# One matmul for gate and up, maxima and exps split by side over three banks each, and the residual add ahead of its maximum

## The chip, the cores and the metric

The kernel runs on one core of one Trainium2 chip. The metric is the device time of one launch in microseconds. TensorE does the matmuls, VectorE, ScalarE and GpSimd the elementwise work, and SyncE issues most DMAs. In the profile they are PE (PEld are its weight loads), DVE, ACT, POOL and SP.

## The reference

One adaLN transformer block over 16 batches of 512 tokens of width 128:

```python
mod = (silu(c) @ wmod).reshape(16, 6, 1, 128)
h = layernorm(x) * (1 + ca) + sa
x = x + ga * attention(h)      # 16 heads of width 8, softmax over 512 keys
h = layernorm(x) * (1 + cb) + sb
x = x + gb * moe(h)            # 8 experts, top 2, hidden width 176
```

The attention is `softmax((h Wq + bq)(h Wk + bk)^T / sqrt(8)) (h Wv + bv)`, then `Wo` and `bo`. An expert is `(silu(h wg) * (h wu)) wd`, and a token's two results are weighted by a softmax over its two best router scores.

## The kernel before, in words

**Attention.** A batch has 16 heads, worked in 4 groups of 4. Two heads make a pair, a "side" each, on rows 0 to 63 and 64 to 127 of TensorE's array. For each pair and each of the 4 tiles of 128 tokens there is a half slot. It has a *score* step two groups ahead of the rest (L808: two matmuls, one for each side, 128 queries by 512 keys; VectorE takes the row maxima of both sides at L1267) and an *exp* step (L817: the two matmuls again, turned and with the maxima as an extra term; ScalarE takes exp at L1038). So there are 32 half slots in a batch. Two of them make one of the 16 slots `k`, and `slot(b, k)` in each engine's program is that engine's share.

TensorE's slot is, in order: scores and exps of half 0, one "misc" step of that slot, scores and exps of half 1, the *value* matmuls (L835, eight records, the weighted sum of the group before), and after every fourth slot the transposed maxima ("shift", L746). `misc_at` says which misc step stands where: slots 1, 5, 9, 13 turn the group's output ("o", L750), 2 the routing places, 3 h2T (L764), 4 v (L742), 6 the router scores (L767), 7 oT, 8 y (L757), 10 x1 (L760), 11 hT (L735), 12 q (L737), 14 k (L739); 0 and 15 have none. All misc steps share bank 7 of PSUM, and each waits until the one before it is drained, mostly by ScalarE between its exps (h_t L995, q and k L999, v_aug L1002, o_t L1004, h2_t L1006, z L1009, shift_n L1017, o_s L1020, and the copy of the value bank, o_aug, L1034). x1 is drained by VectorE: `take_x1` (L1175) adds x into `x1_s`.

**Banks.** PSUM has 8 banks of 512 fp32 columns. Scores use banks 0 to 3 as two areas of two banks, by half slot. Exps use banks 4 and 5 as one area. Bank 6 is for values, bank 7 for misc. TensorE waits before a score step until all maxima but the last step's are done, and before an exp step until all exps are done. The order of work is fixed by the program of each engine. Semaphores `scores_ready`, `maxes_done`, `st_ready`, `exps_done` tie them.

**VectorE beside the maxima.** From slot 6 to slot 11 of a batch it has 16 small router steps of an earlier batch, two per half slot. In slot 11 it has four `bn_stats`.

**Experts.** After attention the 8192 tokens, sorted by expert with GpSimd's indirect DMAs, are worked in 144 tiles of 128 rows: turn the rows (L876), gate and up (L883, two matmuls of 176 columns with the same stationary operand), silu (L1081), product (L1392), turn the hidden rows (L892), down (L900), results back by indirect DMA (L1606). Leftover misc steps of the last batch are mixed into the first tiles. The two halves of the batches are two "superblocks"; the second waits until all its rows are placed.

Of the kernel before, what the change touches and what calls it, by code (L numbers as in the profile page):

```python
# [60 lines left out]
RSTD, NMR, CA, SA, GA, GABO = 0, 4, 8, 9, 10, 11  # L61
PV_BANK, MISC_BANK = 6, 7
XT_BANK, GU_BANK, HT_BANK, Y_BANK = 0, 1, 3, 4
EXP_AREA = 2
STEPS = NH * QT // 2
AHEAD_STEPS = 16

# [57 lines left out]
def along(eng, sem, f, q, d):  # L125

    v = f(q) if d is None else d * (f(q + 1) - f(q)) + f(q)
    if not isinstance(v, int) or v > 0:
        eng.wait_ge(sem, v)

def rows_by_four(v):
# [28 lines left out]
def adaln_block(nc, x, Wq, bq, Wk, bk, Wv, bv, Wo, bo, gate_w, wg, wu, wd, c, wmod,  # L162
                ident_c, tri_c, rank_c, slots_c, map_c, place_c, out):
    with ExitStack() as ctx:
# [36 lines left out]
        mod = sb("mod", [P, 3, NB])  # L201
        gtmp = sb("gtmp", [P, 3, NB])
        row_s = sb("row_s", [NB, ROW_N])
        wg_t = sb("wg_t", [P, NC, P])
        wu_t = sb("wu_t", [P, NC, P])
        wd_t = sb("wd_t", [HALF, 2 * NE, D])
        prm = sb("prm", [P, NB, PRM])
        mv = sb("mv", [P, NT, 2])
# [481 lines left out]
        def _(pe):  # L690
# [37 lines left out]
            def misc_step(kind, n, g, d):  # L728
# [13 lines left out]
                        mm = pe.matmul(misc[:, P * t:P * (t + 1)], h_t[:, P * t:P * (t + 1)], wvT,  # L742
                                       start=True, stop=True)
                elif kind == "shift":
                    wait(pe, maxes_done, lambda n: 2 * GROUP * (NG * n + g + 1), n, d)
                    mm = pe.transpose(misc[0:4 * QT, 0:P], maxes[g % 2][:, :, :, :].rearrange("p a c q -> p (a c q)"), ident[:, :])  # L746
                elif kind == "o":
                    wait(pe, pv_taken, lambda n: NG * n + g + 1, n, d)
# [45 lines left out]
            def slot(b, k, d=None):  # L794
                    g, hh = divmod(k, GROUP)
                    s = NG * b + g
                    exps, looks = 0 <= s < NS, 0 <= s + 2 < NS
                    j, js, bs = 2 * g + hh // 2, (2 * g + hh // 2 + GROUP) % PAIRS, b + (g + 2) // NG
                    for half in range(2):
                        t, step = 2 * (hh % 2) + half, 2 * k + half  # L800
                        if looks:
                            if k == 8 and half == 0:
                                for i in range(2):
                                    wait(pe, stacked[i], lambda b: 16 * STACK_DMAS * (b + 2), b, d)
                            wait(pe, maxes_done, lambda b: STEPS * b + step + AHEAD_STEPS - 1, b, d)
                            for side in range(2):
                                rows = slice(SIDE * side, SIDE * side + SHIFT)
                                mm = pe.matmul(ps[:, 2 * half + side, :], q_st[bs % 2][rows, js, P * t:P * (t + 1)],  # L808
                                               k_st[bs % 2][rows, js, :], start=True, stop=True)
                            mm.then_inc(scores_ready, 1)  # L810
                        if exps:
                            if hh == 0 and half == 0:
                                wait(pe, shift_stacked, lambda b: 32 * (NG * b + g + 1), b, d)
                            wait(pe, exps_done, lambda b: STEPS * b + step, b, d)
                            for side in range(2):
                                rows = slice(SIDE * side, SIDE * side + SHIFT + 2)
                                mm = pe.matmul(ps[:, 2 * EXP_AREA + side, :], k_st[b % 2][rows, j, P * t:P * (t + 1)],  # L817
                                               q_st[b % 2][rows, j, :], start=True, stop=True)
                            mm.then_inc(st_ready, 1)
                        if half:  # L820
                            weigh_values(b, g, hh, d)
                        misc_steps(b, k, half, d)

            def weigh_values(b, g, hh, d):

                s = NG * b + g
                if 0 <= s - 1 < NS:
                    gp, bp = (g - 1) % NG, b + (g - 1) // NG
                    if hh == 0:
                        wait(pe, exps_done, lambda b: 2 * GROUP * (NG * b + g), b, d)  # L830
                        wait(pe, pv_taken, lambda b: NG * b + g - 1, b, d)
                        if gp == 0:
                            wait(pe, misc_drained, lambda b: at["v", b] + 1, b, d)
                    for i in range(GROUP):
                        mm = pe.matmul(ps[VW * i:VW * (i + 1), PV_BANK, :], v_aug[bp % 2][:, hh, GROUP * gp + i, :],  # L835
                                       probs[:, gp % 2, i, S * hh:S * (hh + 1)], start=(hh == 0), stop=(hh == QT - 1))
                    if hh == QT - 1:
                        mm.then_inc(pv_ready, 1)
# [28 lines left out]


            pe.wait_ge(map_step, MAP_STEPS)
            pe.wait_ge(exps_done, STEPS * NB)  # L870

            def turn_rows(m, q, d):

# [4 lines left out]
            def up(m, q, d, e):  # L878

                along(pe, xt_taken, lambda q: PAIR * q + m + 1, q, d)  # L880
                along(pe, hid_ready, lambda q: PAIR * q + m - 1, q, d)
                for i, w in enumerate((wg_t, wu_t)):
                    mm = pe.matmul(ps[:, GU_BANK + m % 2, INTER * i:INTER * (i + 1)], x_t[m % 2],  # L883
                                   w[:, :, :].rearrange("p c h -> p (c h)")[:, bass.ds(e * INTER, INTER)],
                                   start=True, stop=True)
                mm.then_inc(gu_ready, 1)

            def turn_hidden(m, q, d):
                along(pe, hid_ready, lambda q: PAIR * q + m + 1, q, d)
# [61 lines left out]
        def _(act):  # L951
# [20 lines left out]
            def ffn_weights():  # L972
                act.wait_ge(setup_filled, SETUP_MOD2 + 1)
                act.copy(mod_r[:, :, :].rearrange("p a d -> p (a d)"), ps[0:NB, SETUP_MOD2 % 2, 0:3 * D]).then_inc(setup_drained, 1)
                for i, (w, c0, n, width) in enumerate(FFN_GROUPS):
                    act.wait_ge(setup_filled, SETUP_FFN + i + 1)
                    act.copy((wg_t, wu_t, wd_t)[w][:, c0:c0 + n, :].rearrange("p k d -> p (k d)"),
                             ps[0:width, (SETUP_FFN + i) % 2, 0:P * n]).then_inc(setup_drained, 1)

            def prm_of(n):  # L980
# [43 lines left out]
            def slot(b, k, d=None):  # L1024
                    g, hh = divmod(k, GROUP)
                    s = NG * b + g
                    for half in range(2):
# [7 lines left out]
                        if 0 <= s < NS:  # L1035
                            pair_at = 2 * (hh // 2)
                            wait(act, st_ready, lambda b: STEPS * b + step + 1, b, d)
                            act.activation(probs[:, g % 2, pair_at:pair_at + 2, S * t:S * (t + 1)],  # L1038
                                           ps[:, 2 * EXP_AREA:2 * EXP_AREA + 2, :], ACT.Exp, scale=SCALE).then_inc(exps_done, 1)
                        other = misc_at(b, k, half)  # L1040
                        if other and other[0] in ("hT", "q", "k", "v", "oT", "y", "h2T"):
                            misc_drain(*other, d)
# [60 lines left out]
        def _(dve):  # L1103
# [144 lines left out]
            def slot(b, k, d=None):  # L1248
# [3 lines left out]
                    for t in range(QT):  # L1252
                        spot = QT * k + t
                        if 0 <= b - 1 < NB:
# [3 lines left out]
                            if spot == AGGR_AT:  # L1258
                                wait(dve, x1_stats, lambda b: 4 * b, b, d)
                                wait(dve, h2_ready, lambda b: b - 1, b, d)  # L1260
                        if looks and t % 2 == 0:
                            step, tile = 2 * k + t // 2, 2 * (hh % 2) + t // 2
                            area = step % 2
                            if hh == 0 and t == 0 and s >= 0:
                                wait(dve, misc_filled, lambda b: at["shift", NG * b + g] + 1, b, d)
                            wait(dve, scores_ready, lambda b: STEPS * b + step + AHEAD_STEPS + 1, b, d)
                            dve.tensor_reduce(maxes[g % 2][:, :, hh // 2, tile:tile + 1], ps[:, 2 * area:2 * area + 2, :],  # L1267
                                              AX.X, ALU.max).then_inc(maxes_done, 1)
                        other = (misc_at(b, k, 0) if t == 2 else misc_at(b, k - 1, 1) if t == 0 and k else None)
                        if other and other[0] == "x1":  # L1270
                            take_x1(other[1], d)
                        elif other and other[0] == "o":
                            invert_sums(other[1] // NG, other[1] % NG, d)
                        if 0 <= b - 1 < NB:
                            if k == STATS_AT:
# [378 lines left out]
```

## Time and profile before

| | us |
|---|---|
| median of 3 runs | 1164.21 (1160.67 to 1167.68) |
| the profiled execution, own time | 1163.8 |
| its span | 1161.6 |
| PE busy | 985.4 (85%) |
| DVE busy | 865.3 (74%) |
| ACT busy | 794.5 (68%) |
| POOL busy | 677.7 (58%) |

The profile lists busy time by engine, the chain of work that ended last, groups of instructions by line with the idle time before them, and each instruction's start and duration. Attention fills the span to about 877 us, the experts the rest to about 1131, and then come the last sums. "xN" behind a row is how many records are merged in it.

### The profile page before, as it was taken

Reading aid. Unit: us, or ns where it says so; the run is one execution under the profiler, and the core shown is the slowest. Engines: PE = TensorE matmul, PEld = TensorE weight load, DVE = VectorE, ACT = ScalarE, POOL = GpSimd, SP = SyncE. Lnnn points to the kernel's source line nnn. Section 1 sums busy time; section 2 is a strip of 40 time slices with the busy share of each in tenths; the row PEclk is TensorE's granted clock in tenths of the full one; section 3 lists DMA queues with packets and bytes.
Section 4 is the critical chain, followed back from the end, with each engine's and each line's share of the span. In section 5 each row is a group of like instructions: output and inputs, shape, how many; then the busy total and the mean of one; then the engine's idle time right before and its main releaser. Section 6 shows DMA issues by size and latency. Waiting matters only on the chain.

```text
span 1161.6 us, 24273 instructions
## 1 busy us (share of the span) xinstructions
PE 985.4 (85%) x6746; PEld 458.0 (39%) x6747; DVE 865.3 (74%) x1586; ACT 794.5 (68%) x1296; POOL 677.7 (58%) x938
## 2 busy tenths in 40 slices
PE   4778889899898989989898988989788989799990
PEld 2212223223232332323232332323225888689980
DVE  7867788798888979888887978888842554355555
ACT  2367788788778878778787777878675655355550
POOL 6414162857567484856648485664436877765663
PEclk9779999999999999999999999999999999899995
DMA  8211121313112121211122121212022333455566
GB/s 254 76 53 39 38 66 37 84 52 103 51 57 65 56 81 35 83 51 56 52 69 81 35 81 44 65 41 71 11 60 66 81 87 82 123 159 156 168 228 222
DMA packets 98602, 96.32 MB, mean 83 GB/s; under 512 B 21861, under 2 KB 77778, under 8 KB 98514
## 3 DMA queue, kind: packets, MB, share of 16 engines
q1 hardware_dynamic: 89810, 77.34, 23.7%
q0 software_dynamic: 8704, 17.97, 4.5%
q8 instruction: 35, 0.57, 0.2%
q14 instruction: 53, 0.43, 0.1%
HBM read 40.91 MB, written 28.60 MB: 60 GB/s over the span
## 4 chain that ended last, share of the span: by engine, by line
PE 60%; ACT 15%; issue 10%; DVE 7%; SPq 3%; DMA 3%; DVEq 1%; POOL 0%; ACTq 0%
PE ps L835 18%; ACT probs L1038 14%; PE ps L817 11%; PE ps L808 8%; PE ps L883 7%; PE ps L900 5%; PE ps L892 3%; DVE maxes L1267 2%; PE ps L742 1%; PE ps L739 1%; PE ps L737 1%; PE ps L767 1%; PE ps L876 1%; DMA ys_d<-probs,k_st 1%; PE ps L757 1%
## 5 line engine op out<-in xcount | busy, mean ns | idle before, releaser
L1267 DVE TENSOR_REDUCE maxes<-ps 128x2 f32<-128x1024 f32 x512 | 614.3, 1221 | 121.9 <-PE ps L808 116.7
L1038 ACT ACTIVATE probs<-ps 128x1024 f32<-128x1024 f32 x512 | 524.0, 1023 | 152.9 <-PE ps L817 151.0
L835 PE MATMUL ps<-probs,v_aug 128*32 128x512 f32 x2048 | 273.3, 606 | 0.8 <-ACT o_aug L1034 0.8
L817 PE MATMUL ps<-q_st,k_st 64*128 64x512 bf16 x1024 | 200.1, 387 | 79.2 <-ACT probs L1038 77.7
L808 PE MATMUL ps<-k_st,q_st 62*128 62x512 bf16 x1024 | 203.5, 394 | 10.2 <-DVE maxes L1267 9.2
L1493 POOL TENSOR_TENSOR shift_h<-shift_n,one 16x128 bf16<-16x128 f32 x64 | 24.9, 389 | 234.7 <-ACT shift_n L1017 234.7
L1539 POOL DMA_INDIRECT xs_d<-h,rows_o x128 | 125.2, 978 | 35.9 <-issue 35.9
L1388 DVE COPY probs<-ps 88x256 f32<-88x256 f32 x144 | 60.4, 420 | 110.2 <-PE ps L892 107.8
L808 PEld LDWEIGHTS ps<-k_st,q_st 62*128 62x128 bf16 x1024 | 49.3, 93 | 234.8 <-DVE maxes L1267 133.5
L817 PEld LDWEIGHTS ps<-q_st,k_st 64*128 64x128 bf16 x1024 | 50.9, 93 | 175.9 <-ACT probs L1038 147.0
L900 PE MATMUL ps<-wd_t,probs 88*128 x576 | 92.4, 284 | 0.0
L1606 POOL DMA_INDIRECT ys_d<-probs,q_st x72 | 69.7, 969 | 35.6 <-ACT probs L1087 25.9
L1077 ACT COPY probs<-ps 128x128 f32<-128x128 f32 x143 | 38.0, 266 | 74.1 <-PE ps L876 71.1
L1606 POOL DMA_INDIRECT ys_d<-probs,k_st x72 | 70.9, 985 | 29.0 <-ACT probs L1087 17.7
L883 PE MATMUL ps<-wg_t,probs 128*128 x288 | 74.1, 340 | 8.9 <-issue 4.0
L900 PEld LDWEIGHTS ps<-wd_t,probs 88*128 88x128 f32 x576 | 77.2, 195 | 2.9 <-issue 0.2
L1502 POOL TENSOR_TENSOR o_n<-o_s,o_rs 128x128 f32<-128x128 f32 x64 | 27.0, 422 | 86.8 <-DVE o_rs L1167 81.5
L883 PE MATMUL ps<-wu_t,probs 128*128 x288 | 67.9, 318 | 0.0
L835 PEld LDWEIGHTS ps<-probs,v_aug 128*32 128x32 f32 x2048 | 40.4, 108 | 67.8 <-issue 66.1
L892 PE MATMUL ps<-ident,probs 128*88 128x128 f32 x288 | 56.5, 278 | 8.5 <-DVE probs L1392 5.4
L1392 DVE TENSOR_TENSOR probs<-probs,ps 128x176 f32<-128x176 f32 x144 | 46.6, 324 | 10.3 <-ACT probs L1081 10.2
L883 PEld LDWEIGHTS ps<-wu_t,probs 128*128 128x128 f32 x288 | 50.5, 196 | 0.0
(218 smaller groups left out, 1314.5 us busy)
## 6 DMA issues: line engine op xcount, KB each, us to landing
q_st<-q_parts SPq DMA_DIRECT2D x96, 128.0 KB, 2.4
k_st<-k_parts SPq DMA_DIRECT2D x96, 128.0 KB
probs<-ys_d SPq DMA_DIRECT2D x24, 256.0 KB, 3.3
q_st<-xs_d SPq DMA_DIRECT2D x72, 65.0 KB
k_st<-xs_d SPq DMA_DIRECT2D x72, 65.0 KB, 1.9
probs<-L_attn_x SPq DMA_DIRECT2D x4, 1024.0 KB, 8.9
x_r<-L_attn_x SPq DMA_DIRECT2D x16, 256.0 KB, 2.8
x_d<-x_s SPq DMA_DIRECT2D x16, 256.0 KB, 2.1
```

The source lines that it names most:

```text
L808: mm = pe.matmul(ps[:, 2 * half + side, :], q_st[bs % 2][rows, js, P * t:P * (t + 1)], k_st[bs % 2][rows, js, :], start=True, stop=True)
L817: mm = pe.matmul(ps[:, 2 * EXP_AREA + side, :], k_st[b % 2][rows, j, P * t:P * (t + 1)], q_st[b % 2][rows, j, :], start=True, stop=True)
L835: mm = pe.matmul(ps[VW * i:VW * (i + 1), PV_BANK, :], v_aug[bp % 2][:, hh, GROUP * gp + i, :], probs[:, gp % 2, i, S * hh:S * (hh + 1)], s ...
L883: mm = pe.matmul(ps[:, GU_BANK + m % 2, INTER * i:INTER * (i + 1)], x_t[m % 2], w[:, :, :].rearrange("p c h -> p (c h)")[:, bass.ds(e * IN ...
L892: mm = pe.transpose(ps[0:HALF, HT_BANK, P * i:P * (i + 1)], hid[m % 2][:, HALF * i:HALF * (i + 1)], ident[:, :])
L900: mm = pe.matmul(ps[:, Y_BANK + m % 2, 0:D], hid_t[m % 2][:, P * i:P * (i + 1)], wd_t[:, bass.ds(e * 2 + i, 1), :].rearrange("p a d -> p ( ...
L1038: act.activation(probs[:, g % 2, pair_at:pair_at + 2, S * t:S * (t + 1)], ps[:, 2 * EXP_AREA:2 * EXP_AREA + 2, :], ACT.Exp, scale=SCALE).t ...
L1267: dve.tensor_reduce(maxes[g % 2][:, :, hh // 2, tile:tile + 1], ps[:, 2 * area:2 * area + 2, :], AX.X, ALU.max).then_inc(maxes_done, 1)
L1388: dve.tensor_copy(hid_t[(m - 1) % 2], ps[0:HALF, HT_BANK, 0:2 * P]).then_inc(hidt_taken, 1)
L1392: dve.tensor_tensor(hid[m % 2], silu[m % 2], ps[:, GU_BANK + m % 2, INTER:2 * INTER], ALU.mult).then_inc(hid_ready, 1)
L1539: pool.indirect_dma_start(xs_d, bass.IndirectOffsetOnAxis(ap=rows_o[:, v:v + 1], axis=0), h2[n % 2][:, v // QT, v % QT, :], None).then_inc ...
L1606: pool.indirect_dma_start(ys_d, bass.IndirectOffsetOnAxis(ap=x_in[m % SLOTS][:, D + 1:XW].bitcast(U32), axis=0), y_out[m % SLOTS], None).t ...
```

## The change

Three edits. (1) Each score and exp step keeps its two matmuls, but the maxima and the exps are taken in one instruction for each side, of 512 columns instead of 1024. Side 0 of the scores always lands in bank 0, side 1 in banks 1 and 2 by turns; exps likewise in banks 3, 4 and 5. TensorE waits for a score step until side 0 of the step before and side 1 of the one before that are done, and for exps likewise. (2) The gate and up weights lie in one tile `wgu_t`, and one matmul of 352 columns (two runs of 176) takes both. (3) `take_x1` stands ahead of its half slot's maximum, not behind it.

```diff
+SCORE_BANK, EXP_BANK = 0, 3
+def bank_of(first, side, step):
+    return first + 1 + step % 2 if side else first
...
-                            wait(pe, maxes_done, lambda b: STEPS * b + step + AHEAD_STEPS - 1, b, d)
+                            wait(pe, maxes_done, lambda b: 2 * (STEPS * b + step + AHEAD_STEPS) - 1, b, d)
                             for side in range(2):
...
-                                mm = pe.matmul(ps[:, 2 * half + side, :], q_st[bs % 2][rows, js, P * t:P * (t + 1)],
+                                mm = pe.matmul(ps[:, bank_of(SCORE_BANK, side, step), :], q_st[bs % 2][rows, js, P * t:P * (t + 1)],
...
-                            wait(pe, exps_done, lambda b: STEPS * b + step, b, d)
+                            wait(pe, exps_done, lambda b: 2 * (STEPS * b + step) - 1, b, d)
...
-                for i, w in enumerate((wg_t, wu_t)):
-                    mm = pe.matmul(ps[:, GU_BANK + m % 2, INTER * i:INTER * (i + 1)], x_t[m % 2],
-                                   w[:, :, :].rearrange("p c h -> p (c h)")[:, bass.ds(e * INTER, INTER)],
-                                   start=True, stop=True)
-                mm.then_inc(gu_ready, 1)
+                pe.matmul(ps[:, GU_BANK + m % 2, 0:2 * INTER].rearrange("p (a h) -> p a h", a=2), x_t[m % 2],
+                          wgu_t[:, :, :, :].rearrange("p a c h -> p a (c h)")[:, :, bass.ds(e * INTER, INTER)],
+                          start=True, stop=True).then_inc(gu_ready, 1)
...
-                            act.activation(probs[:, g % 2, pair_at:pair_at + 2, S * t:S * (t + 1)],
-                                           ps[:, 2 * EXP_AREA:2 * EXP_AREA + 2, :], ACT.Exp, scale=SCALE).then_inc(exps_done, 1)
+                            for side in range(2):
+                                act.activation(probs[:, g % 2, pair_at + side, S * t:S * (t + 1)],
+                                               ps[:, bank_of(EXP_BANK, side, step), :], ACT.Exp, scale=SCALE).then_inc(exps_done, 1)
...
+                        x1 = misc_at(b, k, 0) if t == 2 else None
+                        if x1 and x1[0] == "x1":
+                            take_x1(x1[1], d)
                         if looks and t % 2 == 0:
...
-                            dve.tensor_reduce(maxes[g % 2][:, :, hh // 2, tile:tile + 1], ps[:, 2 * area:2 * area + 2, :],
-                                              AX.X, ALU.max).then_inc(maxes_done, 1)
+                            for side in range(2):
+                                dve.tensor_reduce(maxes[g % 2][:, side, hh // 2, tile:tile + 1],
+                                                  ps[:, bank_of(SCORE_BANK, side, step), :], AX.X, ALU.max).then_inc(maxes_done, 1)
```

The waits on `maxes_done` and `exps_done` elsewhere count twice as much.

On VectorE, around slot 10 of a batch, the maxima (L1267 before, L1274 now) and the residual add `x_s` (L1175, now L1179) stand as follows. Before:

```order
L1223 TENSOR_TENSOR top<-top 128x4
L118 REGISTER_ALU
L1267 TENSOR_REDUCE maxes<-ps 128x2
L118 REGISTER_ALU x3
L1175 TENSOR_TENSOR x_s<-ps,x_r 128x512
```

Now:

```order
L1227 TENSOR_TENSOR top<-top 128x4
L118 REGISTER_ALU x3
L1179 TENSOR_TENSOR x_s<-ps,x_r 128x512
L118 REGISTER_ALU
L1274 TENSOR_REDUCE maxes<-ps 128x1 x2
```

The add has moved in front of the half slot's maximum, and that is now two instructions, one for each side.

On TensorE, one expert tile among the first (`probs` holds the turned rows, `ISA` and `REGISTER_ALU` are waits and address work). Before:

```order
L883 ISA
L883 MATMUL ps<-wg_t,probs 128x176
L883 REGISTER_ALU
L883 MATMUL ps<-wu_t,probs 128x176
L876 MATMUL ps<-ident,k_st 128x128
```

Now:

```order
L887 ISA
L887 MATMUL ps<-wgu_t,probs 128x352
L881 MATMUL ps<-ident,k_st 128x128
```

Two matmuls and one address step have become one matmul; what stands around them is as it was.

## Rows read from the trace of the kernel before

**Rows 1.** The page's chain that ended last, by engine and by line.

```profile
PE 60%; ACT 15%; issue 10%; DVE 7%; SPq 3%; DMA 3%; DVEq 1%; POOL 0%; ACTq 0%
PE ps L835 18%; ACT probs L1038 14%; PE ps L817 11%; PE ps L808 8%; PE ps L883 7%; PE ps L900 5%; PE ps L892 3%; DVE maxes L1267 2%; PE ps L742 1%; PE ps L739 1%; PE ps L737 1%; PE ps L767 1%; PE ps L876 1%; DMA ys_d<-probs,k_st 1%; PE ps L757 1%
```

**Rows 2.** Busy us of PE, PEld, DVE, ACT, POOL over two batch periods.

```profile
350.85:402.09 51.24, 46.18 (x322) 15.20 (x321) 44.06 (x65) 40.65 (x53) 32.36 (x48) 1.00 0.22 61
95.80:146.10 50.30, 44.30 (x302) 13.37 (x302) 39.26 (x38) 40.17 (x51) 15.74 (x22) 1.00 0.16 46
```

**Rows 3.** The line of h_t, one instruction per batch: durations, first and last start.

```profile
L995 ACT ACTIVATE h_t<-ps,prm_a x15: 774/777/781, 45.0 to 759.5; 128x512 f32<-128x512 f32 x15
```

**Rows 4.** Timeline (start, duration, engine, line), slots 2 and 3 of one batch.

```profile
372.03 1.06 PE L835 MATMUL ps<-probs,v_aug 128*32 128x512 f32 x8
...
373.02 0.39 PE L808 MATMUL ps<-k_st,q_st 62*128 62x512 bf16 x2
...
373.25 0.38 PE L817 MATMUL ps<-q_st,k_st 64*128 64x512 bf16 x2
...
373.46 2.36 DVE L1267 TENSOR_REDUCE maxes<-ps 128x2 f32<-128x1024 f32 x2 [0.59 <-PE ps L808]
...
373.67 1.02 ACT L1038 ACTIVATE probs<-ps 128x1024 f32<-128x1024 f32 x1 [0.51 <-PE ps L817]
...
374.15 0.39 PE L808 MATMUL ps<-k_st,q_st 62*128 62x512 bf16 x2
...
374.59 0.58 ACT L1006 COPY h_t<-ps 128x512 f32<-128x512 f32 x1
...
374.75 0.39 PE L817 MATMUL ps<-q_st,k_st 64*128 64x512 bf16 x2 [0.21 <-ACT probs L1038]
...
375.18 1.02 ACT L1038 ACTIVATE probs<-ps 128x1024 f32<-128x1024 f32 x1
```

**Rows 5.** Timeline of DVE, slots 7 to 12 of the same batch.

```profile
385.99 1.23 DVE L1267 TENSOR_REDUCE maxes<-ps 128x2 f32<-128x1024 f32 x1 [0.21 <-PE ps L808]
387.13 0.18 DVE L1205 TENSOR_REDUCE top<-route 128x4 f32<-128x32 f32 x1
...
388.58 1.64 DVE L1209 TENSOR_TENSOR route<-route,rank 128x32 f32<-128x32 f32 x1
...
399.09 0.68 DVE L1175 TENSOR_TENSOR x_s<-ps,x_r 128x512 f32<-128x512 f32 x1
...
403.31 1.23 DVE L1267 TENSOR_REDUCE maxes<-ps 128x2 f32<-128x1024 f32 x1
```

**Rows 6.** Timeline of PE, slot 11.

```profile
399.90 0.65 PE L735 MATMUL ps<-ident,x_n 128*128 128x128 f32 x4 [1.20 <-DVE x_s L1175]
```

**Rows 7.** The chain in order of time (start, length, what).

```profile
37.50 8.02 DVE maxes L1267 x7
...
351.59 1.05 PE ps L737 x2
...
376.68 1.09 PE ps L742 x8
...
857.89 0.41 PE ps L817 x2
...
859.40 0.41 PE ps L817 x2
...
1060.83 0.64 PE ps L883 x4
...
1062.24 0.64 PE ps L883 x4
```

**Rows 8.** Groups by line and shape, 200 to 800 us.

```profile
L1267 DVE TENSOR_REDUCE maxes<-ps 128x2 f32<-128x1024 f32 x376 | 452.2, 1221 | 83.8 <-PE ps L808 79.2 <-issue 2.0
L1038 ACT ACTIVATE probs<-ps 128x1024 f32<-128x1024 f32 x376 | 384.8, 1023 | 101.1 <-PE ps L817 99.4
...
L1175 DVE TENSOR_TENSOR x_s<-ps,x_r 128x512 f32<-128x512 f32 x11 | 7.5, 680 | 0.0
```

More of the change, by code:

```diff
@@ L63 @@
 XT_BANK, GU_BANK, HT_BANK, Y_BANK = 0, 1, 3, 4
-EXP_AREA = 2
+SCORE_BANK, EXP_BANK = 0, 3
 STEPS = NH * QT // 2
@@ L203, in adaln_block @@
         row_s = sb("row_s", [NB, ROW_N])
-        wg_t = sb("wg_t", [P, NC, P])
-        wu_t = sb("wu_t", [P, NC, P])
+        wgu_t = sb("wgu_t", [P, 2, NC, P])
         wd_t = sb("wd_t", [HALF, 2 * NE, D])
@@ L744, in misc_step @@
                 elif kind == "shift":
-                    wait(pe, maxes_done, lambda n: 2 * GROUP * (NG * n + g + 1), n, d)
+                    wait(pe, maxes_done, lambda n: 4 * GROUP * (NG * n + g + 1), n, d)
                     mm = pe.transpose(misc[0:4 * QT, 0:P], maxes[g % 2][:, :, :, :].rearrange("p a c q -> p (a c q)"), ident[:, :])
@@ L813, in slot @@
                                 wait(pe, shift_stacked, lambda b: 32 * (NG * b + g + 1), b, d)
-                            wait(pe, exps_done, lambda b: STEPS * b + step, b, d)
+                            wait(pe, exps_done, lambda b: 2 * (STEPS * b + step) - 1, b, d)
                             for side in range(2):
                                 rows = slice(SIDE * side, SIDE * side + SHIFT + 2)
-                                mm = pe.matmul(ps[:, 2 * EXP_AREA + side, :], k_st[b % 2][rows, j, P * t:P * (t + 1)],
+                                mm = pe.matmul(ps[:, bank_of(EXP_BANK, side, step), :], k_st[b % 2][rows, j, P * t:P * (t + 1)],
                                                q_st[b % 2][rows, j, :], start=True, stop=True)
@@ L829, in weigh_values @@
                     if hh == 0:
-                        wait(pe, exps_done, lambda b: 2 * GROUP * (NG * b + g), b, d)
+                        wait(pe, exps_done, lambda b: 4 * GROUP * (NG * b + g), b, d)
                         wait(pe, pv_taken, lambda b: NG * b + g - 1, b, d)
@@ L869, in _ @@
             pe.wait_ge(map_step, MAP_STEPS)
-            pe.wait_ge(exps_done, STEPS * NB)
+            pe.wait_ge(exps_done, 2 * STEPS * NB)
             def turn_rows(m, q, d):
@@ L976, in ffn_weights @@
                     act.wait_ge(setup_filled, SETUP_FFN + i + 1)
-                    act.copy((wg_t, wu_t, wd_t)[w][:, c0:c0 + n, :].rearrange("p k d -> p (k d)"),
+                    act.copy((wd_t if w == 2 else wgu_t[:, w, :, :])[:, c0:c0 + n, :].rearrange("p k d -> p (k d)"),
                              ps[0:width, (SETUP_FFN + i) % 2, 0:P * n]).then_inc(setup_drained, 1)
@@ L1260, in slot @@
                                 wait(dve, h2_ready, lambda b: b - 1, b, d)
+                        x1 = misc_at(b, k, 0) if t == 2 else None
+                        if x1 and x1[0] == "x1":
+                            take_x1(x1[1], d)
                         if looks and t % 2 == 0:
                             step, tile = 2 * k + t // 2, 2 * (hh % 2) + t // 2
-                            area = step % 2
                             if hh == 0 and t == 0 and s >= 0:
@@ L1266, in slot @@
                             wait(dve, scores_ready, lambda b: STEPS * b + step + AHEAD_STEPS + 1, b, d)
-                            dve.tensor_reduce(maxes[g % 2][:, :, hh // 2, tile:tile + 1], ps[:, 2 * area:2 * area + 2, :],
-                                              AX.X, ALU.max).then_inc(maxes_done, 1)
+                            for side in range(2):
+                                dve.tensor_reduce(maxes[g % 2][:, side, hh // 2, tile:tile + 1],
+                                                  ps[:, bank_of(SCORE_BANK, side, step), :], AX.X, ALU.max).then_inc(maxes_done, 1)
                         other = (misc_at(b, k, 0) if t == 2 else misc_at(b, k - 1, 1) if t == 0 and k else None)
-                        if other and other[0] == "x1":
-                            take_x1(other[1], d)
-                        elif other and other[0] == "o":
+                        if other and other[0] == "o":
                             invert_sums(other[1] // NG, other[1] % NG, d)
```

## The prediction

> **What bounds the kernel now.** First the chain that ended last [rows 1]: TensorE holds 60% of it (values, exps' and scores' matmuls in front), the exps 14%, the maxima 2%. Then the batch as a unit: h_t comes once per batch, from 45.0 to 759.5 us in 15 instructions, so a period is 714.5 / 14 = 51.0 us [rows 3]. In a late one of 51.24 us PE is busy 46.18, DVE 44.06, ACT 40.65 [rows 2]. No engine is full, so the loss is in handshakes, and the three loads lie so close together that a gain in one soon meets the next.
>
> The handshake is in one slot [rows 4]. With its start (373.02) as 0: scores at 0, exps' matmuls 0.23, maxima 0.44, exp 0.65, misc step 0.54, second scores 1.13. The second exps' matmuls need the exp (1.02) done and start only at 1.73, the values 0.32 later, and they hold PE for 0.99 (372.03 to 373.02): about 3.05 in all. PE idles because exps have one area. Where the misc step is long (q 1.05, v 1.09 [rows 7]) it covers that wait, and such a slot lasts 0.54 + 1.07 + 0.54 + 0.99 = 3.14 already.
>
> Slots 7 to 11 are another regime. DVE starts a maximum of slot 7 at 385.99 and that of slot 12 at 403.31 [rows 5]: 17.32 us for ten maxima with the router's steps between them, one right behind another. There DVE is the bound. PE's wait of 1.20 us for `x_s` at 399.90 [rows 6] lies inside that stretch.
>
> **The price of two instructions for one.** DVE: a maximum of 1024 columns lasts 1.221, and the nearest row of 512 columns out of PSUM is the add, 0.680 [rows 8]. So half a maximum is about 0.68. In a stream the next instruction starts 0.08 before the end of the one in front: 387.13 - 385.99 = 1.14 for 1.23 [rows 5], and two maxima take 2.36, not 2.46 [rows 4]. Two halves take 2 x (0.68 - 0.08) = 1.20 against 1.14, +0.06 a half slot. Bounds: 0 (a half is just half) and 2 x 0.68 - 1.14 = +0.22 (no overlap at all). I take 0.06, since the overlap shows between maxima and between a maximum and small steps alike.
>
> ACT: an exp lasts 1.023 [rows 8], the nearest of 512 columns, the h2_t copy, 0.58, and it starts at 374.59, 0.10 before the exp of 373.67 ends [rows 4]. A pair of half exps is 2 x 0.59 - 0.10 = 1.08, +0.06. Bounds 0 and +0.16.
>
> The rows show a fixed part of about 0.14 in a maximum, of which 0.06 is left in a stream. The Trainium skill (VectorE: DVE Perf Modes, section on the TRN2 errata) puts it at 120 cycles of 0.96 GHz for an operand in PSUM, and says that many small tiles pay it each: an estimated 0.125 us for each added maximum. By that price the result would be near the first rival's.
>
> **What the banks give.** TensorE now waits for side 0 of the step before only. From one exps' matmul to the next: 0.42 until ACT starts (373.25 to 373.67), 0.59 for side 0, 0.05 for the signal, 1.06; it was 1.50. From one score step to the next: 0.44 + 0.68 + 0.05 = 1.17. That is a new limit. Before, PE could be a whole step ahead of DVE, now half of one. Behind a waiting score step stand the exps' matmuls, values and the misc step, which ACT, DVE and the copy of the value bank wait for, so each slot has to be followed on all three engines.
> - A plain slot (13, 15, 1, 2, 3, 5): second scores at 1.17, exps' matmuls at 1.39 (the exp's side 0 ended at 1.24), values at 1.71, end 2.70. Was 3.05: -0.35. DVE needs 2.40 in it, ACT 2 x 0.98. Six of them: -2.1.
> - Slot 0: ACT copies the value bank (0.59) before its first exp, so the second exps' matmuls start at 1.45, plus the shift 0.21: 2.95. With slot 15 it was 6.43, now 5.65; beyond the plain gain of 15 that is -0.4.
> - Slots 6 and 14: PE 3.1 as before, 0.
> - Slot 4: ACT has 1.96 + 0.49 + 0.49 + 0.17 (exps, copy, v, shift) = 3.1 in a slot of 3.37; 0.
> - Slot 12: DVE comes out of slot 11 0.8 behind, so the second scores start at 1.22 + 0.73 = 1.95, not 1.6: 3.7, was 3.53, +0.2.
> - Slots 7 to 11: DVE is the bound, ten half slots by 0.06: +0.6.
> That makes -1.7. The following assumes that no wait meets another, so I take -1.4 a batch, between that and the -1 that is left if every plain slot loses another 0.1. Against DVE's load: 44.06 + 32 x 0.06 = 46.0 of 49.7, no contradiction.
>
> **x ahead of its maximum.** The same DVE work in another order, in the stretch that DVE bounds. PE's hT starts earlier, but its next scores wait for DVE anyway, and the maximum behind the add ends 0.6 later. I take 0; bounds +0.3 and -1.2 a batch, the whole wait of [rows 6].
>
> **Gate and up in one.** Between two tiles lie 1.41 us (1060.83, 1062.24), and gate and up hold 0.64 of it [rows 7]. Four matmuls of 128 columns (v) took 1.09 and one of 512 (q) 1.05 [rows 7]: 0.013 for each matmul saved. Its two passes of records go too, so I take 0.02 x 144 tiles = -3. Bounds: by proportion to the 1.05 of 512 columns the 352 would take 0.72, +0.08 a tile, +12; at best all four records save 0.013, -7. Nothing hides it, since PE bounds the tiles; where the second superblock's rows are waited for, a gain before that is lost.
>
> **The sum**, on the profiled execution's 1163.8 us (span 1161.6), which is 0.4 below the median of 1164.2 and stands for it:
> - 13 periods, slot 11 of batch 1 to slot 11 of batch 14, by 1.4: -18.
> - Two periods before them have no router steps; DVE is busy 39.26 of 50.30 there [rows 2], so slots 7, 9, 10, 11 and 12 gain as plain ones do: 2 x 3.3 = -7.
> - Last batch: slots 12 to 6, -2.2. From slot 8 on no scores are left and the exps alone bound, 857.89 to 859.40, 1.51 a half slot [rows 7]. Now a slot is 1.06 + 0.4 + 0.99 = 2.46, was 3.02: eight times, -4.4.
> - Experts: -3.
> - The first 16 maxima stand alone, 8.02 for 7, 1.15 each [rows 7]; the handshake makes that 1.17 at least, and more at the lower granted clock there: +3.
> Together -31: 1133.
>
> **Rivals.**
> *Halves don't overlap each other*: +0.14 on DVE, +0.16 on ACT a half slot. Slots 7 to 11 lose 1.4, slot 4 and 5 lose 0.4 because ACT runs behind, plain slots keep 0.3: 0 a batch. 1163.8 - 5 - 4 - 3 + 3 = 1155. For it: two instructions on neighbouring banks are not among the pairs that the trace shows. Against: every pair that it does show overlaps.
> *DVE pays the full price*, 0.22: 44.06 + 32 x 0.22 = 51.1 busy; with 1.5 us of idle at score waits 52.6 a period, +1.6. 13 x 1.6 = +21, start +5, last batch -4, experts -3: 1183. It decides from about +0.14 a half slot on. Against it the same rows.
> *The wait for `x_s` is real*: if hT holds slots 11 and 12, another -1.2 a batch, -17: 1116. Against: behind 399.09 DVE has no idle time.
> *Half a step ahead is too little*: what PE no longer waits for ACT it waits for DVE, whose small steps fall between maxima: 1160. For it: DVE's 17.3 us stretch; against: DVE is idle 7 us a period.
>
> **Chances.** Forecast's case (1122 to 1146) 0.50; halves don't overlap 0.18; `x_s` 0.10; too little ahead 0.11; full price 0.11. Less than 0.5% (6 us) can't be told from no change here. Faster: 0.50 + 0.10 + 0.15 of the first rival = 0.75; within: 0.14; slower: 0.11. The range goes from 1114, the `x_s` case, to 1162, past the first and the last rival.
>
> **What would show it.** Half maxima of 0.68 and pairs of 1.28 on DVE; half exps of 0.59, pairs of 1.08; slots 2 and 3 at 2.7, with the second scores waiting for a maximum; slot 7 to 12 on DVE at 18.0; h_t every 49.6; the last batch's exps at 1.2 a half slot; gate and up at 0.62 in a tile of 1.39. The forecast is wrong if h_t still comes every 51 us, if a pair of halves takes 1.36, or if PE's waits for maxima grow by what its waits for exps shrink.

## The result

The changed kernel takes 1146.13 us (median of 4 runs, 1145.74 to 1148.6), the kernel before 1164.22 on the same chip: a ratio of 0.985, with a 95% interval of 0.982 to 0.988. That is 18 us saved. The forecast was 31 us (1133); the time lies inside its range (1114 to 1162), at the very edge of the likeliest case's own (1122 to 1146). The profiled execution took 1146.32, its span 1144.1 against 1161.6, so 17.5 us went out of the span. The ratios with intervals in this text are taken from fast runs alone, and can differ by up to 0.4% from the quotient of the medians beside them.

### The profile after

The page's chain that ended last, as in [rows 1]:

```profile
PE 43%; DVE 20%; issue 13%; POOL 12%; SPq 4%; DMA 4%; ACT 3%; DVEq 1%; POOLq 0%; ACTq 0%
```

GpSimd (POOL) had no share in the chain of before. It has 12% now, and with it SyncE and a DMA. The groups of instructions (busy time and mean ns of one, then the idle time in front and what ended it), first TensorE's two of the kernel before:

```profile
L817 PE MATMUL ps<-q_st,k_st 64*128 64x512 bf16 x1024 | 200.1, 387 | 79.2 <-ACT probs L1038 77.7
L808 PE MATMUL ps<-k_st,q_st 62*128 62x512 bf16 x1024 | 203.5, 394 | 10.2 <-DVE maxes L1267 9.2
```

and of the changed one:

```profile
L1274 DVE TENSOR_REDUCE maxes<-ps 128x1 f32<-128x512 f32 x1024 | 647.7, 683 | 81.4 <-PE ps L813 71.9
L1042 ACT ACTIVATE probs<-ps 128x512 f32<-128x512 f32 x1024 | 559.6, 603 | 128.3 <-PE ps L822 123.7
...
L813 PE MATMUL ps<-k_st,q_st 62*128 62x512 bf16 x1024 | 205.6, 398 | 79.5 <-DVE maxes L1274 76.9
L822 PE MATMUL ps<-q_st,k_st 64*128 64x512 bf16 x1024 | 199.0, 385 | 14.1 <-ACT probs L1042 8.9
```

A half maximum lasts 0.683 us, a half exp 0.603. The matmuls of the scores (L813) now wait for maxima (76.9 us, 9.2 before), and those of the exps (L822) hardly for anything (8.9 us for exps, 77.7 before). Most slots are as forecast. The timeline of slot 15 of one batch, to set beside [rows 4]:

```profile
453.88 1.07 PE L840 MATMUL ps<-probs,v_aug 128*32 128x512 f32 x8
...
454.88 0.39 PE L813 MATMUL ps<-k_st,q_st 62*128 62x512 bf16 x2
455.11 0.38 PE L822 MATMUL ps<-q_st,k_st 64*128 64x512 bf16 x2
455.31 1.89 DVE L1274 TENSOR_REDUCE maxes<-ps 128x1 f32<-128x512 f32 x3 [0.25 <-PE ps L813]
455.53 1.78 ACT L1042 ACTIVATE probs<-ps 128x512 f32<-128x512 f32 x3 [0.34 <-PE ps L822]
456.06 0.39 PE L813 MATMUL ps<-k_st,q_st 62*128 62x512 bf16 x2 [0.57 <-DVE maxes L1274]
456.29 0.38 PE L822 MATMUL ps<-q_st,k_st 64*128 64x512 bf16 x2
456.60 0.64 PE L840 MATMUL ps<-probs,v_aug 128*32 128x512 f32 x4
```

With the slot's start (454.88) as 0: second scores at 1.18, exps' matmuls at 1.41, values at 1.72. From one run of value matmuls to the next it is 456.60 - 453.88 = 2.72, against 3.05 before. The forecast said 1.17, 1.39, 1.71 and 2.70.

And yet the batch gained less than the plain slots promise. The line of h_t, one per batch, as in [rows 3]:

```profile
L998 ACT ACTIVATE h_t<-ps,prm_a x15: 777/783/784, 46.7 to 751.2; 128x512 f32<-128x512 f32 x15
```

The mean period is (751.2 - 46.7) / 14 = 50.3 us, where 51.0 was before and 49.6 was forecast. Two waits that were in no row of before take the difference. The first is on ScalarE, at the start of its loop's body (slot 0 of every second batch; the loop has five rounds, and so four jumps back):

```profile
459.49 0.59 ACT L1037 COPY o_aug<-ps 128x512 f32<-128x512 f32 x1 [1.69 <-issue]
...
460.63 0.39 PE L822 MATMUL ps<-q_st,k_st 64*128 64x512 bf16 x2 [1.46 <-ACT probs L1042]
```

ScalarE sits idle for 1.69 us with nothing that the profile shows to wait for ("issue"), and TensorE then waits 1.46 for its exps. This comes 4 times in the trace, at rounds two to five, 1.54 to 1.79 us each. At the place before, the same copy followed the exp in front of it at once (363.84, behind an exp of 362.74 that lasted 1.02).

The second is in slot 4. The exps' matmuls of a batch's next group need the shift that comes by DMA from GpSimd's `shift_l`. The chain in order of time:

```profile
514.35 1.17 POOL h L1489
...
515.78 0.97 issue
516.74 1.18 POOL h L1492
517.92 0.35 POOL shift_h L1498
...
518.35 0.43 POOL shift_l L1501
...
518.79 0.56 SPq L506
...
519.39 1.61 DMA q_st<-shift_l
...
521.04 0.39 PE ps L822 x2
```

GpSimd's second layer norm (`h`) stands in front of the shift, the shift in front of the DMA, and TensorE stands behind it all. From the start of the shift before it to the end of this one GpSimd takes 18.2 us in both kernels, one instruction right behind the other (406.16 to 424.34 in a batch before, 500.58 to 518.77 here), while TensorE's slots beside it have become shorter. The same layer norm already holds TensorE one slot earlier, at the transposes of h2T, which waited 9 times and 3.9 us in all for `h`:

```profile
517.97 0.66 PE L769 MATMUL ps<-ident,h 128*128 128x128 f32 x4 [0.47 <-POOL h L1492]
```

Over the whole run (idle time of PE and PEld before L822):

```profile
  ACT probs L1042: 28.7, 36
  DMA q_st<-shift_l: 11.5, 17
```

In the trace of before that second releaser doesn't occur at L817: only ACT and "issue" do. Nor does the wait for `h`.

### Where the 17.5 us are

| part of the span | before | after | change | forecast |
|---|---|---|---|---|
| start to the first h_t | 45.0 | 46.7 | +1.7 | +3 |
| 14 periods between h_t | 714.5 | 704.5 | -10.0 | -23 |
| last h_t to the end, without the experts' tiles | 124.2 | 118.2 | -6.0 | -8 |
| experts, first tile to the end | 277.9 | 274.7 | -3.2 | -3 |

The third row is 402.1 - 277.9 and 392.9 - 274.7. The last h_t stands in slot 11 of batch 13, so of the forecast's 15 periods 14 lie between the h_t (2 x 3.3 + 12 x 1.4 = 23.4), and the last belongs to the third row (1.4 + 2.2 + 4.4 = 8.0). The periods missed most of it, by 13 us. The first three gained 0.9, 3.9 and 1.5, the eleven behind them 0.3 on average, and two of those came to 52.4 and 52.3, longer than any of before (51.3).

### The profile page after: what moved, and what is told of

The parts are those of the page before. It is cut to its first block, busy times and chain, and to the rows that moved or that the text cites. A ratio compares the mean times of both kernels' runs of the same rounds, so it can differ in the third digit from the quotient of the medians.

```text
span 1144.1 us, 24592 instructions
## 1 busy us (share of the span) xinstructions
PE 971.6 (85%) x6458; PEld 399.0 (35%) x6459; DVE 894.0 (78%) x2098; ACT 808.0 (71%) x1808; POOL 677.8 (59%) x938
## 4 chain that ended last, share of the span: by engine, by line
PE 43%; DVE 20%; issue 13%; POOL 12%; SPq 4%; DMA 4%; ACT 3%; DVEq 1%; POOLq 0%; ACTq 0%
DVE maxes L1274 15%; PE ps L840 10%; PE ps L813 7%; PE ps L887 6%; PE ps L903 5%; PE ps L822 4%; PE ps L895 3%; POOL rest L1461 2%; ACT probs L1042 2%; PE ps L755 2%; PE ps L747 2%; PE ps L772 1%; DMA q_st<-shift_l 1%; PE ps L881 1%; DVE st_b L1282 1%
## 5 line engine op out<-in xcount | busy, mean ns | idle before, releaser
L1274 DVE TENSOR_REDUCE maxes<-ps 128x1 f32<-128x512 f32 x1024 | 647.7, 683 | 81.4 <-PE ps L813 71.9
L1042 ACT ACTIVATE probs<-ps 128x512 f32<-128x512 f32 x1024 | 559.6, 603 | 128.3 <-PE ps L822 123.7
L813 PE MATMUL ps<-k_st,q_st 62*128 62x512 bf16 x1024 | 205.6, 398 | 79.5 <-DVE maxes L1274 76.9
L822 PE MATMUL ps<-q_st,k_st 64*128 64x512 bf16 x1024 | 199.0, 385 | 14.1 <-ACT probs L1042 8.9
L813 PEld LDWEIGHTS ps<-k_st,q_st 62*128 62x128 bf16 x1024 | 49.4, 93 | 339.6 <-DVE maxes L1274 323.8
L887 PE MATMUL ps<-wgu_t,probs 128*128 x288 | 116.2, 485 | 8.9 <-issue 4.0
L822 PEld LDWEIGHTS ps<-q_st,k_st 64*128 64x128 bf16 x1024 | 51.2, 95 | 33.9 <-ACT probs L1042 19.8
L887 PEld LDWEIGHTS ps<-wgu_t,probs 128*128 128x128 f32 x288 | 43.7, 191 | 11.8 <-issue 11.7
L1085 ACT ACTIVATE probs<-ps 128x176 f32<-128x176 f32 x144 | 46.5, 323 | 0.3 <-PE ps L887 0.3
```

Source lines behind the costliest of these rows:

```text
L813: mm = pe.matmul(ps[:, bank_of(SCORE_BANK, side, step), :], q_st[bs % 2][rows, js, P * t:P * (t + 1)], k_st[bs % 2][rows, js, :], start=Tr ...
L822: mm = pe.matmul(ps[:, bank_of(EXP_BANK, side, step), :], k_st[b % 2][rows, j, P * t:P * (t + 1)], q_st[b % 2][rows, j, :], start=True, st ...
L887: pe.matmul(ps[:, GU_BANK + m % 2, 0:2 * INTER].rearrange("p (a h) -> p a h", a=2), x_t[m % 2], wgu_t[:, :, :, :].rearrange("p a c h -> p ...
L1042: act.activation(probs[:, g % 2, pair_at + side, S * t:S * (t + 1)], ps[:, bank_of(EXP_BANK, side, step), :], ACT.Exp, scale=SCALE).then_i ...
L1274: dve.tensor_reduce(maxes[g % 2][:, side, hh // 2, tile:tile + 1], ps[:, bank_of(SCORE_BANK, side, step), :], AX.X, ALU.max).then_inc(maxe ...
```

## The experiments

They ran on three chips. On two of them every kernel is slower, the one before too (1241.27 and 1257.44 against 1163 to 1164), so only ratios to the kernel before on the same chip are compared. All edits are against the kernel before unless it says otherwise.

### First four: each part by itself

**Gate and up alone.** The edit is the merged matmul of the diff ahead, with `wgu_t` for the two tables.

> The kernel before with the merged gate and up matmul alone. In the trace of the full change the steady tile still takes 1.41 us and gate and up still hold TensorE for 0.64. Theory: TensorE is bound by the 352 streamed columns, not by the number of matmuls, so the steady tile stays at 1.41 and the time moves by at most 1 us, to 1163 to 1164. Rival: the experts' stretch was 3.2 us shorter after the change because a tile behind a stall starts faster (fewer address steps and weight loads), so this kernel gives 3 us, 1161.

Measured: 1232.16 against 1241.27, ratio 0.993 (0.989 to 0.996). Faster by 9 us, more than either of the two expected.

**x ahead of its maximum, alone.** The edit is `take_x1` moved in front.

> The kernel before with the residual add in front of its half slot's maximum alone. Theory (the prediction's): the add lies in the stretch that VectorE bounds, the wait of TensorE for x_s (1.20 us) disappears but the h_t period stays at 51.2 us; within 2 us of 1164. Rival: that wait holds slots 11 and 12, 1.2 us a batch, 14 batches, about 1147.

Measured: 1241.05 against 1241.27, ratio 1.000 (0.996 to 1.003). Nothing, as forecast. TensorE's wait for `x_s` (14.3 us over the run before, PE and PEld together) is gone from this trace, and the time is the same; so the `x_s` rival falls.

**The changed kernel with x behind, as it was.**

```diff
-                        x1 = misc_at(b, k, 0) if t == 2 else None
-                        if x1 and x1[0] == "x1":
-                            take_x1(x1[1], d)
...
+                        if other and other[0] == "x1":
+                            take_x1(other[1], d)
```

> The full change with the residual add put back behind its maximum. Theory: nothing, 1146, within 2 us. Rival: with only half a step of lead the order matters more now; the transposes of hT wait for the add behind two half maxima, about +0.6 us a batch, 1154.

Measured: 1219.3, ratio 0.981 (0.976 to 0.986). Beside the merge alone it is 12.9 us less: that is what the banks of both kinds bring on this chip, with no help from x. The changed kernel itself was not run on this chip, so what the place of x does within it was not compared directly.

**Maxima by side alone, exps as before.**

```diff
-                                mm = pe.matmul(ps[:, 2 * half + side, :], q_st[bs % 2][rows, js, P * t:P * (t + 1)],
+                                mm = pe.matmul(ps[:, bank_of(0, side, step), :], q_st[bs % 2][rows, js, P * t:P * (t + 1)],
...
+                            for side in range(2):
+                                dve.tensor_reduce(maxes[g % 2][:, side, hh // 2, tile:tile + 1],
+                                                  ps[:, bank_of(0, side, step), :], AX.X, ALU.max).then_inc(maxes_done, 1)
```

> The kernel before with the maxima split by side over banks 0 to 2 alone; exps stay one instruction over banks 4 and 5, the matmuls of gate and up stay two. Theory: the gain comes from exps that no longer hold TensorE, and the split maxima only cost (0.06 us a half slot on VectorE in slots 7 to 11, TensorE half a step ahead instead of one): period 51.2 to 52, time 1165 to 1177. Rival: the split maxima give part of the gain themselves: 1155 or less.

Measured: 1261.44, ratio 1.013 (1.008 to 1.018), at or beyond the upper end of what was expected. The splitting of maxima costs 20 us by the medians (16 by the ratio) if the exps stay whole. TensorE is then held on both sides:

```profile
L814 PE MATMUL ps<-k_st,q_st 62*128 62x512 bf16 x1024 | 206.2, 399 | 57.3 <-DVE maxes L1274 52.4
L823 PE MATMUL ps<-q_st,k_st 64*128 64x512 bf16 x1024 | 200.8, 388 | 60.6 <-ACT probs L1044 56.0
```

The distance by which PE may run ahead of DVE has shrunk to half a step, and the wait for the exps is still there. So the gain of the attention part is wholly the exps', and the maxima's half pays for it: it frees the one bank that the exps need beside their two.

### Second four: the two new waits

They ran on a chip where the kernel before takes 1163.07.

**The changed kernel again**, for a measure beside the three that follow.

> The full change once more, unaltered, so that the next three stand beside it on one chip. About 0.985 of the kernel before, as in the first measurement; less time on a chip where the kernel before takes longer because engines wait for instructions.

Measured: 1148.39, ratio 0.986 (0.983 to 0.989).

**ScalarE's loop written out** (the changed kernel; same instructions, no jump back).

```diff
-            with act.Fori(0, LOOP) as d:
-                batch(FIRST, d)
-                batch(FIRST + 1, d)
+            for b in range(FIRST, FIRST + 2 * LOOP):
+                batch(b)
```

> The full change with ScalarE's loop over the middle batches written out, so that it has no branch back. Theory: the four idle times of 1.54 to 1.79 us ahead of the copy of the value bank, once in two batches, are what ScalarE takes to restart its loop; the change exposes them since the loop's last instruction is a short half exp. They go, and with them 6 to 7 us. Rival: ScalarE waits there for new instructions anyway, in a loop or not, and the time stays within 2 us.

Measured: 1144.07, ratio 0.982 (0.979 to 0.985). The idle time is gone (at the same place the copy starts at 458.92, right behind four half exps from 456.72 that lasted 2.27), and the late periods are all 50.4 to 50.5. The gain, 4.3 us, is less than the 6 to 7 expected. But the wait for the shift has grown a little:

```profile
  DMA q_st<-shift_l: 14.1, 21
```

and that of h2T's transposes for `h` too, from 3.9 to 5.0.

**GpSimd's order** (the changed kernel; of the layer norm's five passes the one that only the later scatter needs goes behind the shift).

```diff
-                pool.tensor_tensor(to, to, scale, ALU.mult).then_inc(ln2_step, 1)
+                pool.tensor_tensor(again, to, scale, ALU.mult).then_inc(ln2_step, 1)
...
-                pool.tensor_tensor(again, to, shift_by, ALU.add)
-                pool.tensor_tensor(to, to, shift_by, ALU.add).then_inc(h2_ready, 1)
+                pool.tensor_tensor(to, again, shift_by, ALU.add).then_inc(h2_ready, 1)
...
                 shift_of(b, 1, d)
+                if 0 <= b - 2 < NB:
+                    second_copy(b - 2, d)
```

`second_copy` is the add to `again` that was taken out.

> The full change with GpSimd's second normalisation in another order: the copy that the transposes and nobody else before the scatter needs is made first, then the split of the shift, then the other copy. The same seven operations. Theory: TensorE's exp matmuls of slot 4 wait up to 0.9 us for the DMA of the shift, and the transposes of slot 3 up to 1.0 for GpSimd, because the faster slots 12 to 3 leave GpSimd behind; both waits go, 0.5 to 1 us in each of 13 batches, 6 to 12 us. Rival: those waits are covered by others, within 2 us.

Measured: 1140.23, ratio 0.979 (0.976 to 0.982). PE's and PEld's wait for the shift falls from 11.5 to 1.3 us, h2T's transposes wait for `h` no more, and the idle time at the loop's start stays at 6.5. The periods now alternate, 49.4 and 50.9 to 52.3: the batch with the loop's start is the long one.

**Both.**

> Both edits together, ScalarE's loop written out and GpSimd's order. Theory: they add, 12 to 18 us below the full change. Rival: one wait takes the other's place, no more than the better of the two.

Measured: 1129.6 (1128.77 to 1130.28), ratio 0.970 (0.968 to 0.973), the fastest version on this chip. The same rows as above, of this kernel:

```profile
L998 ACT ACTIVATE h_t<-ps,prm_a x15: 777/783/783, 47.2 to 734.1; 128x512 f32<-128x512 f32 x15
```

```profile
  ACT probs L1042: 15.1, 27
  issue: 3.3, 8
  DMA q_st<-shift_l: 0.7, 4
```

The late periods are all 49.4. Each wait had hidden a part of the other: removed alone they give 4.3 and 8.2 us, removed together 18.8, a little more than the 12 to 18 expected. The 14 periods show the same, 4.2, 7.9 and 16.9 us shorter than in the changed kernel on this chip. In the chain GpSimd is gone again:

```profile
PE 59%; DVE 23%; issue 8%; SPq 4%; DMA 3%; ACT 2%; DVEq 1%; POOL 0%; ACTq 0%
```

### Last four: on a third chip

Here the kernel before takes 1257.44.

**Gate and up alone, again.**

> The merged gate and up matmul alone once more, since its first chip ran everything 7% slower, with waits for instructions in the experts' stretch. Theory: on a chip without those waits only the tiles behind a stall gain, 0 to 3 us of 1164. Rival: the 0.75% of the first measurement holds here too, 9 us.

Measured: 1242.5, ratio 0.986 (0.983 to 0.990), 15 us, again more than either expected.

**Maxima by side alone, again.**

> The split maxima alone once more, for the same reason. Theory: they only cost, 0.6 to 1.6 us in each of 13 batches, 1172 to 1185 where the kernel before takes 1164. Rival: the loss of the first measurement was that chip's; within 2 us.

Measured: 1273.62, ratio 1.012 (1.009 to 1.015). The 1.013 of the other chip repeats, and it is inside what was expected (1172 to 1185 for 1164).

**Exps by side in the two banks that they had.** TensorE waits for each side of its own.

```diff
-                            wait(pe, exps_done, lambda b: STEPS * b + step, b, d)
                             for side in range(2):
+                                wait(pe, exps_done, lambda b: 2 * (STEPS * b + step) - 1 + side, b, d)
...
+                                act.activation(probs[:, g % 2, pair_at + side, S * t:S * (t + 1)],
+                                               ps[:, 2 * EXP_AREA + side, :], ACT.Exp, scale=SCALE).then_inc(exps_done, 1)
```

> The kernel before with exps split by side in their two old banks: TensorE's matmul of a side waits for that side's exp only. Scores and their maxima stay as they were. Theory: without the third bank the second side's matmul waits until side 1 is done, 1.14 + 0.59 after the first exp's start, as late as the whole exp before, so a plain slot stays at 3.05 and ScalarE has 0.06 a half slot more to do: 1160 to 1170. Rival: splitting the instruction is enough, and the banks are not needed: 1145 or less.

Measured: 1290.49, ratio 1.025 (1.021 to 1.028). The loss was not expected, only that nothing would be gained. Smaller instructions without a third bank bring no gain, since the second side's matmul stands still in the middle of the pair. In the timeline:

```profile
357.25 0.82 PE L817 MATMUL ps<-q_st,k_st 64*128 64x512 bf16 x2
...
358.00 1.07 PE L834 MATMUL ps<-probs,v_aug 128*32 128x512 f32 x8
...
359.22 0.38 PE L817 MATMUL ps<-q_st,k_st 64*128 64x512 bf16 x2
```

The pair that waits for side 1 lasts 0.82 instead of 0.38, and the value matmuls stand behind it. Slots 10 and 11 are 3.09 to 3.10 long (354.90, 358.00, 361.09), and 3.05 in the kernel with the merge alone on the same chip (351.71, 354.76, 357.80). But 0.05 a slot is less than 1 us a batch, and the 14 periods are together 30 us longer than there (776.1 against 746.0). The larger part stands elsewhere: ScalarE is idle 2.05 to 2.25 us at each of its loop's four later rounds, and slot 8 of that batch lasts 6.85 where the other kernel has 4.90, with waits that have no known releaser. So 1.025 isn't the price of the missing bank alone, and how much of it is was not separated.

**All loops written out** (both edits of the fastest version, and the attention's loops of all five engines flat).

> The version with ScalarE written out and GpSimd's order, with the loops of TensorE, VectorE, GpSimd and SyncE over the middle batches written out as well. Theory: the other engines' branches back are covered, so within 3 us of 0.970 of the kernel before, a little more if longer programs are waited for. Rival: each branch costs as ScalarE's did, and another 3 to 8 us go.

Measured: 1199.28, ratio 0.954 (0.950 to 0.957). That is 0.016 under the 0.970 expected, and more than the rival's further 3 to 8 us too. Late periods are 49.8 to 53.3. The fastest version itself was not run on this chip, so how much of the 58 us is owed to the four other loops stays open.

## Why the prediction was right, and where it missed

**What held.** The mechanism is the forecast's, and its rivals fall. A pair of half maxima takes 1.28 to 1.29 us and four in a row 2.48, so +0.06 a half slot; a pair of half exps 1.08 to 1.09. The rival "halves don't overlap each other" wanted 1.36, "DVE pays the full price" is out with it, and the `x_s` rival by the second experiment. DVE's busy time for maxima is 647.7 us in the changed kernel and 614.3 in the one before: 33.4 / 512 = 0.065 a half slot. The Trainium skill (VectorE: DVE Perf Modes, section on the TRN2 errata) gives a VectorE instruction with its source in PSUM 120 cycles beside its columns, at 0.96 GHz an estimated 0.125 us for each added one; its sentence that many small tiles pay per tile is said of SBUF's latency. The measured 0.065 decides: about half of that price is left when halves follow each other. For the exps, the Trainium skill (ScalarE: Activation LUTs, "What ACT_TABLE_LOAD costs") says that back-to-back activations overlap by about 93 ns; the trace has 2 x 0.603 - 1.09 = 0.12.

**Slots.** Plain ones came to 2.72 (forecast 2.70). Slots 7 to 11 stretched on DVE from 17.32 to 497.49 - 479.89 = 17.60 us, +0.28 where +0.6 (18.0) was forecast, and slot 12 by the +0.2 of the forecast.

```profile
479.89 1.29 DVE L1274 TENSOR_REDUCE maxes<-ps 128x1 f32<-128x512 f32 x2
...
497.49 1.29 DVE L1274 TENSOR_REDUCE maxes<-ps 128x1 f32<-128x512 f32 x2
```

The last batch's exps go at 2.40 a slot (forecast 2.46). The rows of the chain there:

```profile
856.94 0.39 PE ps L822 x2
857.33 0.99 PE ps L840 x8
858.33 0.34 PE ps L822 x2
858.67 0.02 issue
858.69 0.61 ACT probs L1042
859.30 0.05 issue
859.35 0.39 PE ps L822 x2
```

**The step that failed** is the line "The following assumes that no wait meets another, so I take -1.4 a batch". The slots were followed on PE, DVE and ACT and on the copy of the value bank, and not on the engines that feed them once a group. Over the twelve periods with router steps the changed kernel gained 5.3 us where 16.8 were forecast, so it lost about 1 us of the 1.4 in a batch. It lost them to two things that TensorE had not waited for before: the start of ScalarE's loop, and GpSimd's layer norm with the shift behind it. The first belongs to the half exps: idle time at that copy with no releaser stands 4 times in each kernel that halves them and has ScalarE's loop (6.7, 6.4, 6.2 and 6.5 us in all with three banks, 8.6 with two), and not once in the six runs with whole exps. Why half exps bring it out was not tested: they are shorter, but the loop's body also has more instructions (over the run ScalarE has 1808 by the page where exps are halved, 1296 before). The experiments settle both waits as the cause of the lost periods: with both taken away the late period is 49.4, against 49.6 forecast, the 14 periods give -27.6 against -23.4, and the kernel is at 1129.6. That the forecast named 1133 for the unmended kernel was wrong; for the mended one it would have been nearly right.

**A sign that misled.** The forecast was to be wrong if PE's waits for maxima grew by what its waits for exps shrank. That came about almost exactly: +67.7 us (9.2 to 76.9) against -68.8 (77.7 to 8.9), and the fastest version has 77.1 and 3.1. The time fell all the same, because PE's busy time fell too, from 46.18 in the period of [rows 2] to 45.20 in one of the fastest version. In a plain slot before, the second exps' matmuls started 0.60 behind their scores' with idle time between (374.15 and 374.75 in [rows 4]), and now 0.23 behind them without any (456.06 and 456.29). So the sum of idle times at two lines isn't a measure of the period.

**The first period** gained 0.9 us where 3.3 was forecast (49.9 against 50.8), and it is 49.5 to 50.0 long in the four runs on the second fast chip too. The granted clock in it was 0.74 of full before and 0.69 after, while the forecast's plain slots are from stretches at 1.00. What bounds it was not looked into.

**A limit on the mended version.** The two edits were made to the changed kernel alone. What they would give the kernel before was not run; its trace shows neither wait, which makes a gain there unlikely but doesn't measure it.

**The experts.** The term of -3 came out (3.2), but not by its reason, and perhaps by luck: the same tiles take 274.3 to 277.3 us in the four runs on the second fast chip, against 277.9 before, so one trace of each can't tell 3 from 0.6. The tile in a steady stretch is what it was:

```profile
1040.18 0.64 PE ps L887 x2
1040.82 0.11 PE ps L881
1040.93 0.22 PE ps L895 x2
1041.15 0.45 PE ps L903 x4
1041.60 0.64 PE ps L887 x2
```

1041.60 - 1040.18 is 1.42, with the rounding the 1.41 of [rows 7], and gate and up still hold 0.64, in 352 columns as in twice 176. The "0.02 a tile" doesn't exist, and the +0.08 of its upper bound doesn't either. What may gain are tiles behind an interruption, where PE catches up with instructions that it hadn't yet been given. That is a reading and not shown. It fits the two slower chips, where such interruptions are many: from the first tile to the end the four kernels with two matmuls take 326.0 to 338.7 us there, the four merged ones 319.5 to 322.4. Weight loads of gate and up waited there with no releaser shown, in the kernel with x moved alone:

```profile
L883 PEld LDWEIGHTS ps<-wg_t,probs 128*128 128x128 f32 x288 | 46.1, 201 | 47.9 <-issue 47.0
```

and in the merged one:

```profile
L881 PEld LDWEIGHTS ps<-wgu_t,probs 128*128 128x128 f32 x288 | 46.3, 201 | 40.1 <-issue 39.8
```

In the kernel before, on its chip, the same wait is 11.5 us. But it is 45.1 in the merged kernel with x behind, on the same slow chip, so this wait by itself doesn't carry the gain. The merge brings 9 and 15 us on the slow chips, and the experts' part gives 4.8 of the 9 (326.0 with x alone moved, 321.2 merged); where the rest comes from was not found. On the fast chip the merge was not run alone.

**The first maxima.** The first h_t came 1.7 us later and not 3. In the four runs of versions with the same start on the second fast chip it came 2.1 to 3.5 later than in the trace of before, so this term can't be told from its forecast.

**Chances.** Faster by over 0.5% had 0.75 and is what came. The rival "half a step ahead is too little" (1160) is nearest in place to what happened, since PE does wait for DVE in most slots now (76.9 us at the scores), but it is refuted as the reason of the miss: that wait is the same 77.1 in the fastest version.

## What stays open

Exps by side in three banks with the maxima whole would tell the two halves apart fully. It needs seven banks beside the value and misc banks, nine where PSUM has eight, so it would need another layout and wasn't tried. The merge alone wasn't run on a fast chip, nor the two mending edits on the kernel before, and the changed kernel and the fastest version weren't run on a slow one.

## What to carry to other kernels

When an instruction is split so that its producer may start earlier, count the buffers: the split pays with a third bank (a plain slot of 2.72 us against 3.05) and doesn't without one (3.10). When a period shrinks, list everything that arrives once per period, on the engines off the path too, with the time by which each is early: what was early by less than the gain becomes the new bound. And two such waits hide each other, so mend both before you judge either (4.3 and 8.2 us alone, 18.8 together).

## What the runs showed of the hardware

- At each jump back of its loop ScalarE is idle for 1.54 to 1.79 us in the kernels with half exps in three banks (0.60 us each) and 2.05 to 2.25 with half exps in two, for nothing that shows in those with whole ones (1.02), and for nothing when the loop is written out.
- One fp32 matmul of 352 columns and two of 176 hold TensorE for the same 0.64 us in a steady stream.
- Of two chips, the same kernel is 7 to 8% slower than on the others (1241 and 1257 against 1163), at like durations of single instructions (a whole maximum 1.222 us, an exp 1.024) and with more waits that have no releaser in the profile. Between those two the maxima alone gave the same ratio (1.013 and 1.012), and the merge alone 0.993 and 0.986.
